# The queries of a wide cross-attention: two contexts' first, the other fourteen's inside the first chunk-maximum pass

## The chip, the cores and the metric

The kernel runs on one core of one Trainium2 chip. The metric is the device time of one execution in microseconds, the median of three runs. The engines that matter are PE (TensorE, matmuls, with PEld its weight loads), DVE (VectorE), ACT (ScalarE), POOL (GpSimd) and SP, which issues most DMAs. Each has its own instruction queue and they meet only through semaphores and at the end of a block.

## The reference, cut to what matters

Four gated layers follow each other, each a cross-attention and a feed-forward part. The change is in the cross-attention of the second layer (L1) alone. x is 32 batches of 56 queries by 128; the context of a batch is 1500 rows by 96; 16 heads of 64.

```python
q = (x @ Wq).reshape(B, Nq, h, dh)          # x: layer-normed, 32 x 56 x 128
k = (context @ Wk).reshape(B, Nk, h, dh)    # context: 32 x 1500 x 96
v = (context @ Wv).reshape(B, Nk, h, dh)
scores = einsum('bqhd,bkhd->bhqk', q, k) / sqrt(dh)
attn = softmax(scores, axis=-1)
out = einsum('bhqk,bkhd->bqhd', attn, v).reshape(B, Nq, h * dh) @ Wo + bo
```

## The kernel before, in words

`attention_wide` first folds the weights (`fold_weights`): for each head Wq and Wk become one matrix M of 128 by 97, so that a "query" of 96 numbers meets the raw context directly; N does the same for Wv and Wo. Then it runs two halves of 16 contexts each. The program text calls a context a batch.

A half has two blocks. In the first, `make_queries` makes the queries of all 16 contexts: for two stretches c of 448 columns (8 contexts) and for 16 heads, one fp32 matmul (two passes of PE each, L527) into one of eight PSUM banks; ACT copies the even heads (L544) and DVE the odd ones (L557) into `qp`, scaled and with a bias. Beside it SP issues the loads of contexts 0 and 1 (`raw`, `cn`) and POOL issues four more (`cr`, then `ch`) and fills a row of ones. A block ends when all its engines have ended.

In the second block, contexts go two at a time (`i` is the pair, `s` which of the two), in a software pipeline written out by hand:

- POOL rounds the queries to `QB` (L1255) and splits queries and keys into high and low parts (`QH` L1265, `CL` L1269, `QL` L1271). It also issues the DMA that puts a row of maxima into `QH` (`max_row`, L1276).
- First pass, `chunks` on PE (L1328): queries times rounded keys, 11 groups for a context, ten of two matmuls of 500 columns and one of one. DVE takes each group's maximum (`chunk_max`, L1509), and after 11 groups the negated maximum of the row (L1514, L1517).
- `score` (L1351 to L1353, six matmuls of 448 columns for one key tile) needs that row through `max_row`. ACT takes the exponential (L1491), `weigh` (L1365) multiplies by the context's values.
- `project` (L1336, 16 heads, two passes each) and an ACT copy (L1429) end a pair.

For the pair 0 of a half the first pass stands ahead of the loop, alone on PE, with two pairs of PSUM banks (0 and 1, 6 and 7):

```python
pe.wait_ge(S["ones_set"].sem, 2 * half + 2)
for s in range(2):
    for k in range(CG):                    # CG = 11
        chunks(0, s, k, True)
pe.wait_ge(*at("chunk_maxed", 2 * CG))
score(0, 0)
score(0, 1)
pairs(pe, body)
```

POOL, before it reaches its loop, waits for each context's 11 groups, rounds the queries of pair 1 and issues their keys' load, and only then issues the first `max_row`. From the loop's start on, the first pass of pair i + 1 lies between the scores of pair i. ACT's queue in the second block begins with two loads of a stored image and one operation on it (L1444); then it waits for the first score.

Of the kernel before, what the change touches and what calls it, by code (L numbers as in the profile page):

```python
# [19 lines left out]
ALU = mybir.AluOpType  # L20
# [3 lines left out]
B, NQ, D = 32, 56, 128  # L24
# [30 lines left out]
class Core:  # L55
# [27 lines left out]
    def new_signals(self, later=False):  # L83

        nc, old = self.nc, self.signals
        if later:
            self.done += old
        elif old:
            with nc.Block() as block:
                @block.gpsimd  # L90
                def _(pool):
                    nc.clear_and_free_semaphores([s.sem for s in old])
        self.signals = []
        self.part += 1
        self.step = {e: self.sig(f"{e}_step") for e in ("dve", "act", "pe", "pool")}
        self.queries_made, self.queries_act, self.queries_dve = (
            self.sig(f"queries_{n}") for n in ("made", "act", "dve"))
        self.gate_added = self.sig("gate_added")
        self.mean_ready = self.sig("mean_ready")
        self.centred = self.sig("centred")  # L100
        self.squared = self.sig("squared")
        self.var_ready = self.sig("var_ready")
        self.std_ready = self.sig("std_ready")
        self.inverse_ready = self.sig("inverse_ready")
        self.inverse_spread = self.sig("inverse_spread")
# [402 lines left out]
                                            ALU.mult).then_inc(m_sb.sem, 1)  # L508


def make_queries(core, qp, M, cq, src, scale, half, loads, rounded_loads):

    nc, ps = core.nc, core.ps
    qmm, qa, qd_ = core.queries_made, core.queries_act, core.queries_dve
    nch = NCH // 2
    with nc.Block() as block:
        block.sync(loads)
        block.gpsimd(rounded_loads)

        @block.tensor  # L520
        def _(pe):
            with pe.Fori(0, nch) as c:
                for h in range(H):

                    w = qa if h % 2 == 0 else qd_
                    pe.wait_ge(w.sem, w.at(8 * c + h // 2 + 1))
                    nc.tensor.matmul(ps[0:KA, h % 8, 0:CH], M[:, h, :],  # L527
                                     src[:, bass.ds(c * CH + half * nch * CH, CH)],
                                     start=True, stop=True).then_inc(qmm.sem, 1)

        def bank(h):
            return ps[0:KA, h % 8, 0:CH].rearrange("p (b q) -> p b q", q=NQ)

        def place(h, c):
            return qp[0:KA, bass.ds(c * 8, 8), h * NQ:(h + 1) * NQ]

        @block.scalar
        def _(act):
            act.sem_inc(qa.sem, 4)
            with act.Fori(0, nch) as c:  # L540
                for h in range(0, H, 2):
                    act.wait_ge(qmm.sem, qmm.at(H * c + h + 1))
                    if cq is not None:
                        ins = nc.scalar.activation(place(h, c), bank(h), ACT.Identity,  # L544
                                                   bias=cq[:, h:h + 1], scale=scale)
                    else:
                        ins = nc.scalar.activation(place(h, c), bank(h), ACT.Copy)
                    ins.then_inc(qa.sem, 1)

        @block.vector  # L550
        def _(dve):
            dve.sem_inc(qd_.sem, 4)
            with dve.Fori(0, nch) as c:
                for h in range(1, H, 2):
                    dve.wait_ge(qmm.sem, qmm.at(H * c + h + 1))
                    if cq is not None:
                        ins = nc.vector.tensor_scalar(place(h, c), bank(h), scale, cq[:, h:h + 1],  # L557
                                                      ALU.mult, ALU.add)
                    else:
                        ins = nc.vector.tensor_copy(place(h, c), bank(h))  # L560
                    ins.then_inc(qd_.sem, 1)
    qmm.base += H * nch
    qa.base += H * nch // 2 + 4
    qd_.base += H * nch // 2 + 4

PRODUCTS = [(0, 0), (0, 1), (1, 0), (1, 1), (0, 2), (2, 0)]
# [22 lines left out]
def attention_normed(core, L, qn, bo, rk, bit, image):  # L595
# [10 lines left out]
    with ExitStack() as ctx:  # L606
# [486 lines left out]
        "den_out": 32 * NP, "den_stored": 32 * NP, "den_in": 32 * NP, "den_inverted": 2 * NP,  # L1093
        "u_normed": 2 * NP + 1, "projected": NP, "out_copied": NP,
        "img_in": 96 * NP, "img_valued": 6 * NP, "img_scaled": 6 * NP, "img_rounded": 6 * NP,
        "img_made": 6 * NP, "img_kept": 6 * NP, "img_seen": 6 * NP, "img_out0": 48 * NP, "img_out1": 48 * NP}
IMAGE_AT = (1, 4, 7, 13, 16, 19)


def attention_wide(core, L, src, bo, scale, bit, image, norm):  # L1100

    outer = ExitStack()
    N = core.sb(f"{L}_N", [KA, H, D], F32, outer)
    M = core.sb(f"{L}_M", [D, H, KA], F32, outer)
    cq = core.sb(f"{L}_cq", [KA, H], F32, outer)
    S = {n: core.sig(f"{L}_{n}") for n in [*WIDE, "ones_set"]}
    with outer:
        fold_weights(core, L, M, N, cq, scale, True, 64, None, norm)
        for half in range(2):
            with ExitStack() as ctx:  # L1110
                qp = core.sb(f"{L}_qp{half}", [DC + 8, HB, HQ], F32, ctx)

                def queries(loads, rounded_loads):
                    make_queries(core, qp, M, cq, src, scale, half, loads, rounded_loads)
                attend_wide(core, f"{L}{half}", S, qp, N, bo, half, ctx, bit, image, queries)


def attend_wide(core, tag, S, qp, N, bo, half, ctx, bit, image, queries):

# [2 lines left out]

    nc, d, ps = core.nc, core.d, core.ps
    b0 = half * HB

    def at(name, n):
        return S[name].sem, S[name].at(n)

    def sb(name, shape, dt=F32):
        return core.sb(f"{tag}_{name}", shape, dt, ctx)
# [87 lines left out]
        for s in range(2):  # L1220
            nc.gpsimd.tensor_copy(CH[s][DC:KA, :], core.ones[DC:KA, 0:1].to_broadcast([1, NK])).then_inc(S["ones_set"].sem, 1)

    queries(loads, rounded_loads)
    with nc.Block() as block:
        @block.sync
        def _(sp):
            def invert(i, s):

                sp.wait_ge(*at("u_copied", 2 * i + s + 2))

                sp.dma_start(dn, UE[DC:KA, :]).then_inc(S["den_out"].sem, 16)
                sp.wait_ge(*at("den_inverted", 2 * i + s + 1))
                sp.dma_start(den.rearrange("o (t n) -> (o t) n", t=8), dr).then_inc(S["den_stored"].sem, 16)
                sp.wait_ge(*at("den_stored", 32 * i + 16 * s + 16))
                sp.dma_start(RB[:, :], den.to_broadcast([DC, HQ])).then_inc(S["den_in"].sem, 16)

            def body(i, prev, nxt, after):
                if prev:
                    invert(i - 1, 1)
                for s in range(2):  # L1240
                    if nxt:
                        sp.wait_ge(*at(f"keys_split{s}", 3 * i + 3))
                        raw_keys(sp, i + 1, s)
                        sp.wait_ge(*at("weighed", 24 * i + 12 * s + 14))
                        rows(sp, i + 1, s)
                    if s == 0:
                        invert(i, 0)

            pairs(sp, body)
            invert(NP - 1, 1)  # L1250

        @block.gpsimd
        def _(pool):
            def first_pass_inputs(i, s, keys=True):
                nc.gpsimd.tensor_copy(QB[s][:, :].rearrange("c (t p) -> c t p", p=128),  # L1255
                                      folded(i, s).rearrange("c (p t) -> c t p", p=128)
                                      ).then_inc(S[f"qb_ready{s}"].sem, 1)
                if keys:
                    first_pass_keys(pool, i, s)
# [14 lines left out]
            def max_row(i, s):  # L1274
                pool.wait_ge(*at("max_negated", 2 * i + s + 1))
                pool.dma_start(QH[s][DC:KA, :], negated(i, s)).then_inc(S[f"max_in{s}"].sem, 16)  # L1276
# [10 lines left out]
            for s in range(2):  # L1287

                pool.wait_ge(*at("chunk_scored", CG * s + CG))
                first_pass_inputs(1, s)  # L1290
            max_row(0, 0)

            def body(i, prev, nxt, after):
                max_row(i, 1)
# [18 lines left out]
        def _(pe):  # L1313
# [76 lines left out]
            def body(i, prev, nxt, after):  # L1390
                for k in range(24):
# [15 lines left out]
                    if k % KT == 0:  # L1407
                        aside(i, k, prev, nxt)
                        weigh(i, k)

            pe.wait_ge(S["ones_set"].sem, 2 * half + 2)
            for s in range(2):
                for k in range(CG):
                    chunks(0, s, k, True)
            pe.wait_ge(*at("chunk_maxed", 2 * CG))
            score(0, 0)
            score(0, 1)
            pairs(pe, body)
            pe.wait_ge(*at("u_normed", 2 * NP))
# [3 lines left out]
        def _(act):  # L1423
# [36 lines left out]
            def image_step(i, n, prev, nxt):  # L1460

                for c, k in enumerate(IMAGE_AT):
# [6 lines left out]
                    if n == k + 4 and (c < 4 or nxt):  # L1469
                        j = (i, c + 2) if c < 4 else (i + 1, c - 4)  # L1470
                        act.wait_ge(*at("img_valued", 6 * i + c + 2))
                        load_image(*j)

            load_image(0, 0)
            value(0, 0, False)
            act.wait_ge(*at("img_valued", 1))
            load_image(0, 1)

            def body(i, prev, nxt, after):
                for n in range(24):  # L1480
# [2334 lines left out]
```

## Time and profile before

| what | us |
|---|---|
| median of 3 runs (lowest, highest) | 4207.23 (4205.37, 4211.37) |
| profiled execution | 4212.35 |
| its span from first to last instruction | 4210.4 |
| PE, DVE, ACT, POOL busy in the span | 3661.9, 2545.5, 2041.4, 1477.9 |
| queries of the first half, L527, first to last matmul | 26.07 |
| queries of the second half, L527 | 26.71 |

Times within the trace count from the span's start. In a timeline row, the first two numbers are start and length; `x4` is how many instructions were merged; the bracket tells how long the engine had been idle before and what ended that. In the table of stretches, PEclk is the granted share of TensorE's full clock: 1.00 is 2.4 GHz, 0.50 is 1.2 GHz. Ends of matmuls are modelled, so the spacing of their starts is the better measure.

### The profile page before, as it was taken

Reading aid. Unit: us, or ns where it says so; the run is one execution under the profiler, and the core shown is the slowest. Engines: PE = TensorE matmul, PEld = TensorE weight load, DVE = VectorE, ACT = ScalarE, POOL = GpSimd, SP = SyncE. Lnnn points to the kernel's source line nnn. Section 1 sums busy time; section 2 is a strip of 40 time slices with the busy share of each in tenths; the row PEclk is TensorE's granted clock in tenths of the full one; section 3 lists DMA queues with packets and bytes.
Section 4 is the critical chain, followed back from the end, with each engine's and each line's share of the span. In section 5 each row is a group of like instructions: output and inputs, shape, how many; then the busy total and the mean of one; then the engine's idle time right before and its main releaser. Section 6 shows DMA issues by size and latency. Waiting matters only on the chain. (4 is left out here: it accounts for less than half of the span.)

```text
span 4210.4 us, 84369 instructions
## 1 busy us (share of the span) xinstructions
PE 3661.9 (87%) x33096; PEld 2477.5 (59%) x33096; DVE 2545.5 (60%) x3583; ACT 2041.4 (48%) x2943; POOL 1477.9 (35%) x1913
## 2 busy tenths in 40 slices
PE   8499999937489999988999997679858799999987
PEld 8267777724446666655666665357633366666664
DVE  7556666535155554525554542467644799999995
ACT  8177777701024443432443342166422477777764
POOL 5275455130423323212223220022201666666640
PEclk9599999969679999998999997889979799999998
DMA  6177777446223233221332220021000666666650
GB/s 185 48 177 178 169 176 172 120 184 231 47 70 93 82 86 85 79 66 55 85 88 85 83 76 25 9 63 48 10 19 26 138 156 154 156 155 155 155 131 25
DMA packets 201964, 436.40 MB, mean 104 GB/s; under 512 B 46666, under 2 KB 103917, under 8 KB 201517
## 3 DMA queue, kind: packets, MB, share of 16 engines
q1 hardware_dynamic: 127196, 341.47, 31.3%
q0 software_dynamic: 38944, 47.04, 5.2%
q10 hardware_dynamic: 35504, 43.39, 3.8%
q8 instruction: 230, 3.77, 0.4%
q14 instruction: 90, 0.73, 0.1%
HBM read 246.72 MB, written 32.67 MB: 66 GB/s over the span
## 5 line engine op out<-in xcount | busy, mean ns | idle before, releaser
L1509 DVE TENSOR_REDUCE L_mp<-ps 128x2 f32<-128x1000 f32 (+1 forms) x352 | 403.4, 1152 | 554.7 <-PE ps L1328 551.3
L1491 ACT ACTIVATE L_p<-ps 125x896 f32<-125x896 f32 x384 | 352.1, 917 | 606.2 <-PE ps L1353 534.5
L1365 PE MATMUL ps<-L_p,L_cn 125*97 125x448 f32 x1536 | 639.2, 538 | 0.0
L2196 ACT ACTIVATE L_p<-L_p 125x896 f32<-125x896 f32 x384 | 364.5, 950 | 226.4 <-DVE L_p L2257 222.6
L2240 DVE TENSOR_REDUCE L_mp<-ps 112x2 f32<-112x1000 f32 x384 | 455.4, 1190 | 18.2 <-PE ps L2002 18.1
L2257 DVE SCALAR_TENSOR_TENSOR L_p<-ps,xn 125x896 f32<-125x896 f32 x384 | 414.0, 1080 | 16.8 <-PE ps L2022 16.5
L1351 PE MATMUL ps<-L_qh,L_ch 97*125 97x448 f32 x768 | 385.8, 502 | 14.6 <-DMA L_qh<-L_mc 14.6
L1365 PEld LDWEIGHTS ps<-L_p,L_cn 125*97 125x97 f32 x1536 | 250.4, 163 | 199.9 <-issue 165.9
L2002 PE MATMUL ps<-L_ks,L_qs 96*128 96x500 bf16 x768 | 236.2, 392 | 78.8 <-DVE L_mp L2240 65.5
L1352 PE MATMUL ps<-L_ql,L_ch 96*125 96x448 f32 x768 | 284.0, 370 | 0.0
L1353 PE MATMUL ps<-L_qh,L_cl 96*125 96x448 f32 x768 | 282.5, 368 | 0.0
L946 ACT ACTIVATE L_p<-ps,rk 125x896 f32<-125x896 f32 x256 | 257.5, 1007 | 51.1 <-PE ps L802 46.9
L1328 PE MATMUL ps<-L_cr,L_qb 96*128 96x500 f32 x672 | 242.2, 443 | 13.3 <-DVE L_mp L1509 7.2
L1777 POOL DMA_DIRECT2D L_qs<-L_q_part x381 | 211.7, 564 | 99.4 <-PE ps L2022 93.0
L2022 PEld LDWEIGHTS ps<-L_qs,L_ks 128*128 128x128 bf16 x3072 | 188.9, 98 | 74.5 <-issue 45.2
L802 PEld LDWEIGHTS ps<-L_qs,L_ks 128*128 128x128 bf16 x3072 | 188.1, 98 | 72.9 <-issue 54.4
L2035 PE MATMUL ps<-L_p,L_vs 125*18 125x112 f32 x6144 | 223.2, 263 | 3.5 <-ACT L_p L2196 3.1
L802 PE MATMUL ps<-L_qs,L_ks 128*128 128x112 bf16 x3072 | 216.1, 213 | 3.4 <-ACT L_p L946 3.4
L728 POOL DMA_DIRECT2D L_qs<-L_q_part x384 | 214.3, 566 | 7.6 <-DVEq L1068 6.8
L2022 PE MATMUL ps<-L_qs,L_ks 128*128 128x112 bf16 x3072 | 215.1, 213 | 1.5 <-DVE L_p L2257 1.0
L1280 POOL TENSOR_TENSOR L_un<-L_ue,L_rb 96x896 f32<-96x896 f32 x32 | 67.1, 2097 | 423.6 <-DMA L_rb<-L_den 423.6
L718 POOL TENSOR_TENSOR L_k_part<-L_k_rest,L_k_part 128x500 bf16<-128x500 f32 x96 | 109.2, 1139 | 300.3 <-ACT L_k_part L911 300.2
(537 smaller groups left out, 7299.8 us busy)
## 6 DMA issues: line engine op xcount, KB each, us to landing
L_ks<-L_k_part SPq DMA_DIRECT2D x288, 375.0 KB, 6.6
L_ks<-L_k_first SPq DMA_DIRECT2D x96, 375.0 KB, 6.3
moe_w<-in_L_w SPq DMA_DIRECT2D x64, 512.0 KB, 6.6
L_cn<-in_ctxN SPq DMA_DIRECT2D x32, 568.4 KB
cs_ct<-in_ctxT SPq DMA_DIRECT2D x32, 562.5 KB, 4.2
L_raw<-in_ctxT SPq DMA_DIRECT2D x32, 562.5 KB, 4.8
L_cr<-in_ctxT POOLq DMA_DIRECT2D x32, 562.5 KB, 5.0
L_ch<-in_ctxT POOLq DMA_DIRECT2D x32, 562.5 KB, 4.5
```

Source lines behind the costliest of these rows:

```text
L802: mm = nc.tensor.matmul(SB[n % 2][:, m // 4, m % 4 * 2 * NQ:(m % 4 + 1) * 2 * NQ] .rearrange("p (j q) -> p j q", j=2), KS[b.r % 3][:, k0:k ...
L946: nc.scalar.activation(weights_at[n % 3][0:KP, :].rearrange("p (a n) -> p a n", a=2), SB[n % 2][0:KP], ACT.Exp, scale=rk[:, b.lin(KT, n):b ...
L1351: nc.tensor.matmul(SB[n % 2][:, a, :], CH[s][:, k], QH[s][:, q], start=True, stop=False)
L1352: nc.tensor.matmul(SB[n % 2][:, a, :], CH[s][0:DC, k], QL[s][:, q], start=False, stop=False)
L1353: mm = nc.tensor.matmul(SB[n % 2][:, a, :], CL[s][:, k], QH[s][0:DC, q], start=False, stop=True)
L1365: mm = nc.tensor.matmul(U[:, a, :], CN[s][:, j, :], P[:, n % 2, a * HALF:(a + 1) * HALF], start=(j == 0), stop=(j == KT - 1))
L1491: nc.scalar.activation(two(P[:, n % 2, :]), SB[n % 2], ACT.Exp).then_inc(S["exped"].sem, 1)
L1509: nc.vector.tensor_reduce(mp[:, 2 * k:2 * k + n], ps[:, bank:bank + n, 0:500], AX.X, ALU.max).then_inc(S["chunk_maxed"].sem, 1)
L2022: mm = nc.tensor.matmul(SB[n % 2][:, m // 4, m % 4 * 2 * NQ:(m % 4 + 1) * 2 * NQ] .rearrange("p (j q) -> p j q", j=2), KS[b.r % 4][:, k0:k ...
L2196: nc.scalar.activation(two(P[0:KP, n % 3, :]), two(P[0:KP, n % 3, :]), ACT.Exp).then_inc(S["exped"], 1)
L2240: nc.vector.tensor_reduce(mp[:, 2 * c:2 * c + 2], ps[0:TT, CB[pair], 0:500], AX.X, ALU.max).then_inc(S["chunk_maxed"], 1)
L2257: nc.vector.scalar_tensor_tensor(out=two(P[0:KP, n % 3, :]), in0=SB[n % 2][0:KP], scalar=0.0, in1=two(LB[0:KP, b.r % 2, :]), op0=ALU.min, ...
```

## The change

`make_queries` is replaced by `first_queries`, which in the first block makes the queries of contexts 0 and 1 only: 16 matmuls of 112 columns into banks 0 to 3, four heads to a bank, with no loop; ACT copies heads 0 to 3 and 8 to 11, DVE the others, each after its four heads. POOL's four loads and its row of ones stay in that block. SP's four loads move into the second block and wait there until `cr` of context 1 has landed.

The queries of the other 14 contexts are made in the second block by 32 matmuls of 392 columns (`late_query`, 7 contexts by 16 heads, twice). One stands behind each of the 22 chunk groups of pair 0 in PE's queue, the last ten behind those. They use banks 2 to 5; from the fifth on each waits for the copy of the one four before. ACT alone copies them, behind its image operation. The second score waits for all 32 copies; POOL waits for 16 copies before it rounds the queries of pair 1, and for all 32 before its loop. The bias row of 97 becomes 96 rows (the 97th was not used in `qp`).

```diff
-def make_queries(core, qp, M, cq, src, scale, half, loads, rounded_loads):
+def first_queries(core, S, qp, M, cq, src, scale, half, rounded_loads):
...
+            for h in range(H):
+                nc.tensor.matmul(ps[0:DC, h // 4, h % 4 * 2 * NQ:(h % 4 + 1) * 2 * NQ], M[:, h, 0:DC],
+                                 src[:, b0 * NQ:(b0 + 2) * NQ], start=True, stop=True
+                                 ).then_inc(S["early_made"].sem, 1)
...
+            for h in (h for h in range(H) if h // 4 % 2 == 0):
+                act.wait_ge(*at("early_made", h // 4 * 4 + 4))
+                nc.scalar.activation(place(h), bank(h), ACT.Identity, bias=cq[0:DC, h:h + 1], scale=scale)
...
+            for h in (h for h in range(H) if h // 4 % 2 == 1):
+                dve.wait_ge(*at("early_made", h // 4 * 4 + 4))
+                nc.vector.tensor_scalar(place(h), bank(h), scale, cq[0:DC, h:h + 1], ALU.mult, ALU.add)
...
+LATE_BATCHES = (HB - 2) // 2
...
+            sp.wait_ge(*at("ctr_in1", 16))
+            loads(sp)
...
                 pool.wait_ge(*at("chunk_scored", CG * s + CG))
+                pool.wait_ge(*at("late_copied", H))
                 first_pass_inputs(1, s)
             max_row(0, 0)
+            pool.wait_ge(*at("late_copied", 2 * H))
...
+            def late_query(e):
+                if e >= 4:
+                    pe.wait_ge(*at("late_copied", e - 3))
+                c = (b0 + late_batches(e)) * NQ
+                nc.tensor.matmul(ps[0:DC, 2 + e % 4, 0:LATE_BATCHES * NQ], M[:, e % H, 0:DC], src[:, c:c + LATE_BATCHES * NQ],
+                                 start=True, stop=True).then_inc(S["late_made"].sem, 1)
...
                     chunks(0, s, k, True)
+                    late_query(CG * s + k)
+            for e in range(2 * CG, 2 * H):
+                late_query(e)
             pe.wait_ge(*at("chunk_maxed", 2 * CG))
             score(0, 0)
+            pe.wait_ge(*at("late_copied", 2 * H))
             score(0, 1)
...
+            def copy_late_query(e):
+                act.wait_ge(*at("late_made", e + 1))
+                n, h = late_batches(e), e % H
+                nc.scalar.activation(qp[0:DC, n:n + LATE_BATCHES, h * NQ:(h + 1) * NQ],
+                                     ps[0:DC, 2 + e % 4, 0:LATE_BATCHES * NQ].rearrange("p (b q) -> p b q", q=NQ),
+                                     ACT.Identity, bias=cq[0:DC, h:h + 1], scale=scale
+                                     ).then_inc(S["late_copied"].sem, 1)
...
+            for e in range(2 * H):
+                copy_late_query(e)
```

## Rows read from the trace of the kernel before

**Rows 1.** The page, part 1: busy time and share of each engine.
```profile
PE 3661.9 (87%) x33096; PEld 2477.5 (59%) x33096; DVE 2545.5 (60%) x3583; ACT 2041.4 (48%) x2943; POOL 1477.9 (35%) x1913
```
**Rows 2.** Timeline of the first half's start: start, length, engine, line, instruction, idle before.
```profile
1163.91 26.07 PE L527 MATMUL ps<-xn,L_M 128*97 x64 [0.88 <-ACTq L539]
...
1191.11 3.57 POOL L1255 CAST L_qb<-L_qp 96x896 fp32r<-96x896 f32 x2 [22.07 <-POOLq L516]
1193.03 1.14 PE L1328 MATMUL ps<-L_cr,L_qb 96*128 96x500 f32 x4 [3.05 <-POOL L_qb L1255]
1193.75 2.31 DVE L1509 TENSOR_REDUCE L_mp<-ps 128x2 f32<-128x1000 f32 x2 [2.94 <-PE ps L1328]
...
1195.65 3.36 POOL L1269 TENSOR_TENSOR L_cl<-L_raw,L_ch 96x1500 fp32r<-96x1500 f32 x1
1196.24 2.31 DVE L1509 TENSOR_REDUCE L_mp<-ps 128x2 f32<-128x1000 f32 x2 [0.19 <-PE ps L1328]
...
1218.61 0.79 PE L1328 MATMUL ps<-L_cr,L_qb 96*128 96x500 f32 x1 [0.18 <-DVE L_mp L1509]
1219.47 1.77 POOL L1255 CAST L_qb<-L_qp 96x896 fp32r<-96x896 f32 x1 [9.83 <-PE ps L1328]
...
1226.87 0.71 PE L1351 MATMUL ps<-L_qh,L_ch 97*125 97x448 f32 x1 [7.48 <-DMA L_qh<-L_mc]
```
**Rows 3.** Timeline of the loop's first steps, PE alone.
```profile
1231.49 1.02 PE L1328 MATMUL ps<-L_cr,L_qb 96*128 96x500 f32 x2
1232.32 0.39 PE L1351 MATMUL ps<-L_qh,L_ch 97*125 97x448 f32 x1
...
1233.57 1.67 PE L1365 MATMUL ps<-L_p,L_cn 125*97 125x448 f32 x4
...
1238.51 0.61 PE L1328 MATMUL ps<-L_cr,L_qb 96*128 96x500 f32 x2
1238.96 1.67 PE L1365 MATMUL ps<-L_p,L_cn 125*97 125x448 f32 x4
```
**Rows 4.** Timeline around the start of the second half.
```profile
1867.78 7.14 PE L1336 MATMUL ps<-L_un,L_N 96*128 96x112 f32 x32 [10.15 <-POOL L_un L1280]
...
1875.99 26.71 PE L527 MATMUL ps<-xn,L_M 128*97 x64 [1.07 <-ACTq L539]
...
1903.83 3.54 POOL L1255 CAST L_qb<-L_qp 96x896 fp32r<-96x896 f32 x2 [22.90 <-POOLq L516]
```
**Rows 5.** Stretches: length, busy time of PE, PEld, DVE, ACT, POOL, PEclk, DMA share, GB/s.
```profile
1163.50:1167.50 4.00, 3.59 (x5) 1.55 (x6) 0.11 (x1) 0.63 (x1) 3.42 (x5) 0.50 0.74 187
1167.50:1190.00 22.50, 22.48 (x60) 9.51 (x58) 10.16 (x15) 9.50 (x15) 1.53 (x2) 1.00 0.72 173
1195.00:1219.00 24.00, 21.64 (x38) 9.74 (x38) 22.44 (x22) 0.96 (x1) 14.47 (x8) 0.50 0.19 54
1227.00:1232.00 5.00, 5.00 (x14) 4.38 (x15) 0.00 (x0) 1.19 (x2) 0.00 (x0) 0.50 0.00 0
1867.00:1875.00 8.00, 7.14 (x32) 6.90 (x32) 0.00 (x0) 0.04 (x1) 0.64 (x1) 0.50 0.00 0
3600.00:3700.00 100.00, 92.25 (x1345) 61.56 (x1336) 98.46 (x102) 70.45 (x112) 59.89 (x106) 1.00 0.71 161
1232.00:1840.00 608.00, 608.00 (x2413) 408.93 (x2412) 296.11 (x381) 248.91 (x346) 161.74 (x109) 1.00 0.28 79
```
**Rows 6.** Groups by line: busy, mean ns of one, idle before.
```profile
L544 ACT ACTIVATE L_qp<-ps,L_cq 97x448 f32 x32 | 20.3, 633 | 59.5 <-PE ps L527 59.5
L1429 ACT ACTIVATE OT<-ps,vec 128x112 f32 (+1 forms) x16 | 5.7, 353 | 94.3 <-PE ps L1336 94.3
L1018 DVE SCALAR_TENSOR_TENSOR OT<-ps,vec,OT 128x112 f32<-128x112 f32 x16 | 5.2, 323 | 3.5 <-PE ps L843 3.5
```
**Rows 7.** DMA issues at 1163.9, and at 1209: count, KB, us to landing.
```profile
L_cr<-in_ctxT POOLq DMA_DIRECT2D x1, 562.5 KB, 11.1
...
L_cr<-in_ctxT POOLq DMA_DIRECT2D x1, 562.5 KB, 4.5
```

More of the change, by code:

```diff
@@ L95, in new_signals @@
         self.step = {e: self.sig(f"{e}_step") for e in ("dve", "act", "pe", "pool")}
-        self.queries_made, self.queries_act, self.queries_dve = (
-            self.sig(f"queries_{n}") for n in ("made", "act", "dve"))
         self.gate_added = self.sig("gate_added")
@@ L508, in _, with at, bank, place @@
                                             ALU.mult).then_inc(m_sb.sem, 1)
-def make_queries(core, qp, M, cq, src, scale, half, loads, rounded_loads):
+def first_queries(core, S, qp, M, cq, src, scale, half, rounded_loads):
     nc, ps = core.nc, core.ps
-    qmm, qa, qd_ = core.queries_made, core.queries_act, core.queries_dve
-    nch = NCH // 2
+    b0 = half * HB
+    def at(name, n):
+        return S[name].sem, S[name].at(n)
+    def bank(h):
+        return ps[0:DC, h // 4, h % 4 * 2 * NQ:(h % 4 + 1) * 2 * NQ].rearrange("p (b q) -> p b q", q=NQ)
+    def place(h):
+        return qp[0:DC, 0:2, h * NQ:(h + 1) * NQ]
     with nc.Block() as block:
-        block.sync(loads)
         block.gpsimd(rounded_loads)
@@ L521, in _ @@
         def _(pe):
[L522 to L532, printed above, removed]
@@ L534, in place @@
-        def place(h, c):
-            return qp[0:KA, bass.ds(c * 8, 8), h * NQ:(h + 1) * NQ]
+            for h in range(H):
+                nc.tensor.matmul(ps[0:DC, h // 4, h % 4 * 2 * NQ:(h % 4 + 1) * 2 * NQ], M[:, h, 0:DC],
+                                 src[:, b0 * NQ:(b0 + 2) * NQ], start=True, stop=True
+                                 ).then_inc(S["early_made"].sem, 1)
         @block.scalar
         def _(act):
[L539 to L548, printed above, removed]
+            for h in (h for h in range(H) if h // 4 % 2 == 0):
+                act.wait_ge(*at("early_made", h // 4 * 4 + 4))
+                nc.scalar.activation(place(h), bank(h), ACT.Identity, bias=cq[0:DC, h:h + 1], scale=scale)
@@ L550, in _ @@
         @block.vector
         def _(dve):
[L552 to L561, printed above, removed]
@@ L562, in make_queries @@
-    qmm.base += H * nch
-    qa.base += H * nch // 2 + 4
-    qd_.base += H * nch // 2 + 4
+            for h in (h for h in range(H) if h // 4 % 2 == 1):
+                dve.wait_ge(*at("early_made", h // 4 * 4 + 4))
+                nc.vector.tensor_scalar(place(h), bank(h), scale, cq[0:DC, h:h + 1], ALU.mult, ALU.add)
 PRODUCTS = [(0, 0), (0, 1), (1, 0), (1, 1), (0, 2), (2, 0)]
@@ L1095 @@
         "img_in": 96 * NP, "img_valued": 6 * NP, "img_scaled": 6 * NP, "img_rounded": 6 * NP,
+        "early_made": H, "late_made": 2 * H, "late_copied": 2 * H,
         "img_made": 6 * NP, "img_kept": 6 * NP, "img_seen": 6 * NP, "img_out0": 48 * NP, "img_out1": 48 * NP}
 IMAGE_AT = (1, 4, 7, 13, 16, 19)
+LATE_BATCHES = (HB - 2) // 2
 def attention_wide(core, L, src, bo, scale, bit, image, norm):
@@ L1111, in attention_wide, with attend_wide, late_batches @@
                 qp = core.sb(f"{L}_qp{half}", [DC + 8, HB, HQ], F32, ctx)
[L1113 to L1118, printed above, removed]
+                attend_wide(core, f"{L}{half}", S, qp, (M, cq, src, scale), N, bo, half, ctx, bit, image)
+def attend_wide(core, tag, S, qp, query, N, bo, half, ctx, bit, image):
     nc, d, ps = core.nc, core.d, core.ps
     b0 = half * HB
+    M, cq, src, scale = query
     def at(name, n):
         return S[name].sem, S[name].at(n)
+    def late_batches(e):
+        return 2 + LATE_BATCHES * (e // H)
     def sb(name, shape, dt=F32):
@@ L1221, in rounded_loads @@
             nc.gpsimd.tensor_copy(CH[s][DC:KA, :], core.ones[DC:KA, 0:1].to_broadcast([1, NK])).then_inc(S["ones_set"].sem, 1)
-    queries(loads, rounded_loads)
+    first_queries(core, S, qp, M, cq, src, scale, half, rounded_loads)
     with nc.Block() as block:
```

## The prediction

> **What bounds the kernel now.** I read the shares of the engines first. PE is busy for 87% of the span [rows 1], so the question for any stretch is whether PE is the bound there, and at which clock. The table of stretches answers it [rows 5]: from 1232 to 1840, the loop of the first half, PE is busy 608.00 of 608.00 us at PEclk 1.00. In the loop only less PE work saves time, and the change takes none out of it. The rest I read from the timeline ahead of the loop, because that is where the edit lies.
>
> There the kernel is serial. In the first half PE makes queries from 1163.91 on, and POOL, which needs only the first two contexts' queries, begins to round them at 1191.11, when the whole block has ended [rows 2]: 27.20 us. In the second half it is 1875.99 to 1903.83 [rows 4]: 27.84 us. PE sets this stretch: 60 passes fill 22.48 of 22.50 us, 0.375 us each, at clock 1.00 [rows 5].
>
> Behind it comes the first pass of pair 0, 1193.03 (first chunk matmul) to 1226.87 (first score), 33.84 us. Here the end is set by DVE and by PE's latency in turn: two maxima take 2.31 us, then DVE idles 0.19 us for PE, and the next two start 2.49 us after the first (1193.75, 1196.24) [rows 2]. The clock is 0.50 from 1195 to 1219 [rows 5]. A pair of chunk matmuls takes 0.83 us there (that of 1231.49 to 1232.32, still at the low level) and 0.45 us at the high one (1238.51 to 1238.96) [rows 3]. So at 1.2 GHz PE has work for 0.83 of each 1.25 us, and ACT and SP have next to none: ACT is busy 0.96 us of 24 [rows 5]. The last chunk starts at 1218.61; then POOL rounds once more (1219.47, 1.77 us), issues `max_row`, and PE idles 7.48 us before the score [rows 2].
>
> **The change, part by part.**
>
> *First block.* Removed per half: 27.20 and 27.84 us. In its place 16 matmuls of 112 columns, 32 passes. `project` has just these, 32 passes of 112 columns in 7.14 us [rows 4], at clock 0.50 [rows 5]. I take 7.14, since the block starts at 0.50 [rows 5] and `project` did not raise the clock in as much time. Copies of three groups of heads lie beside PE; the last group's four by DVE come after it, at 0.323 us each, the nearest row with 112 columns read from PSUM [rows 6]: 1.29. ACT's last four end earlier: 0.353 each [rows 6], begun a quarter of 7.14 us before. Hand-over costs about 0.3 us on both sides of them (an estimate: 0.72 us from chunk to maximum [rows 2] less 0.45 for the pair [rows 3]). Sum 7.14 + 1.29 + 0.6 = 9.0. Gain 18.2 and 18.8 us. Bounds: passes at half that price (3.6), or at the 0.407 us of a full pass (26.07/64 [rows 2], 13.0 in all): 5.9 us less to 3.5 us more gain in a half.
>
> *Loads.* `cr` of context 0 landed 11.1 us after its issue when it shared the DMA engines with SP's four loads; alone it takes 4.5 [rows 7]. Now SP's stand behind it, so it lands near 1169, before the rounded queries (9.0 + 1.8 us after 1163.91, about 1174.7). If it still took 11.1 it would land at 1175.2 and cost 0.5. `raw` starts some 10 us later; POOL wants it for `CL` 4.5 us after its first rounding [rows 2]. Even a late `raw` delays only POOL's splitting: 14.47 us of POOL work between 1195 and 1219 [rows 5], the later rounding included, wanted by a score 33 us after the first chunk. Cost 0.
>
> *Chunks with 22 late queries among them.* A late query is two passes of 392 columns: 2 x 0.375 x 392/448 = 0.66 us at clock 1.00, 1.31 at 0.50. With its chunk pair PE needs 1.11 us a group at 2.4 GHz, 2.14 at 1.2. So the clock decides. What raises it in this trace: full-width passes back to back, after 4 us in the query block (0.50 to 1167.5, then 1.00) and after 5 us of scores (0.50 to 1232, then 1.00); what keeps it: 92.25% busy from 3600 to 3700 at 1.00 [rows 5]. With a query behind each group PE has no pause at 1.2 GHz, so I expect the rise after 4 to 5 us and then 1.00. In those, PE does two groups, where DVE did 3.5; I put the loss at 2.4 us. Then PE (1.11) and DVE (1.11 when maxima run back to back: 2.31 for two with 1.20 for the last) go level, against 1.25 before: 18 full groups by 0.14 win 2.5 back. Net next to nothing; I book a loss of 0.3 us. Bounds: a gain of 2, and the first rival.
>
> *Tail.* The query behind the last group and the ten after it are 11 x 0.66 = 7.2 us. POOL's round and `max_row` hide it: the score came 7.48 us after PE's last chunk [rows 2]. Nothing moves, with some 0.5 us to spare. ACT's copies lie between 0.353 (112 columns) and 0.633 us (448) [rows 6], by the line through both 0.59 for 392, below PE's 0.66, four banks deep. Were the tail at 1.2 GHz it would take 14.4 and cost 7 a half. POOL's added wait for 16 copies ends with group 16, before its wait for 22; its wait for 32 holds back only the `max_row` of the second context, needed twelve key tiles later.
>
> *Scores that start at full clock.* PE no longer idles for 7 us before the first score. The twelve matmuls of the first two scores and the chunk pair behind them took 1226.87 to 1232.32, 5.45 us, at clock 0.50 [rows 2, 3, 5]. In the loop six scores take 1.25 us (1232.32 to 1233.57) and the pair 0.45 [rows 3]: 2.95 us. Gain at most 2.5, I take 2.3; zero if the clock falls.
>
> *Sum.* First half 18.2 - 0.3 + 2.3 = 20.2, second 20.8: 41.0 us. The profiled execution took 4212.35 us, so 4171.3 for it; it lay 5.1 over the median of the runs, and against the median the same step gives 4207.23 - 41.0 = 4166.2.
>
> **The rivals.**
>
> *The clock stays low (slower).* Between 1195 and 1219 PE counts as 21.64 us busy of 24 and had 0.50 all the while [rows 5], so a nearly busy PE is not proof of a high clock. If it stays at 1.2 GHz until the first score, PE is the bound: 20 groups of 2.14, two short ones of 1.73, ten queries of 1.31, 59.4 us where 33.84 were: +25.5 a half. Against 18.2 and 18.8 that is 14 us slower, 4221. It decides from about seven tenths of the phase at 1.2 GHz on. Against it: the same trace rises in every stretch where full-width matmuls stand without pauses. The Trainium skill ("TensorE: Matmul & The Clock Gate", "A second HAM failure mode: psum-queue depth-cycling") reports a kernel that, going round PSUM banks, paused so often that its clock fell and rose again and again; by that rule this is the case. The 92% of 3600 to 3700 speak against it here.
>
> *The clock is high only in part.* It rises late or falls once, for instance when PE meets DVE's pause at the change of context, and the tail or a third of the phase runs at 1.2 GHz: 7 to 9 us a half. Gain 23 to 27, about 4182. For it: level PE and DVE leave no reserve.
>
> *The gain is given back.* Something that the long query block covers becomes the wait, such as the contexts that SP reads later, or the image load ahead of ACT's copies in the same DMA traffic, and all of it is lost: 4207. Priced by the 11.1 us of a load in traffic [rows 7], ACT begins to copy some 3 us after PE wants its first bank back, 3 us a half, far from all; and the loop behind, PE from end to end, gives back nothing.
>
> **How the numbers follow.** Forecast 4166, chance 0.70, its own range 4156 to 4176 (bounds of the first block and no gain in the scores). Clock in part 0.14; slower by the clock 0.06; given back or not done 0.05; a larger gain, by a faster first block, 0.05. Differences under 0.2% (8.4 us) can't be told from none. Faster 0.89, the same 0.05, slower 0.06. The range of 8 in 10 reaches into the partial clock: 4156 to 4187.
>
> **What would show it.** Right: POOL's first rounding about 9 us after the first query matmul; PEclk 1.00 from some 5 us after the first chunk; maxima 1.1 to 1.2 us apart; first score 33 to 35 us after the first chunk, its matmuls 0.2 us apart; the loop as long as before. Wrong: 0.50 in the chunk stretch, chunk groups 2 us apart, a score that waits for copies rather than for `max_row`, or a first block of over 13 us.

## The result, and the profile after

The changed kernel takes 4169.23 us (4166.84 to 4173.88) against 4208.06 (4205.37 to 4211.37) for the one before on the same chip: ratio 0.9905, interval [0.9894, 0.9917]. The forecast was 4166, faster. The sum is near, but its largest term was not: errors of both signs partly cancel.

The timeline of the changed kernel at the first half's start, engine by engine, in the columns of [rows 2]:

```profile
1159.77 5.17 PE L529 MATMUL ps<-xn,L_M 128*96 128x112 f32 x32 [0.53 <-PEq L468]
...
1164.99 1.06 DVE L543 TENSOR_SCALAR L_qp<-ps,L_cq 96x112 f32<-96x112 f32 x4 [0.84 <-PE ps L529]
1171.95 0.34 SPq L1172 DMA_DIRECT2D L_raw<-in_ctxT  x1
1171.96 3.52 POOL L1235 CAST L_qb<-L_qp 96x896 fp32r<-96x896 f32 x2 [6.71 <-POOLq L523]
...
1173.88 1.17 PE L1310 MATMUL ps<-L_cr,L_qb 96*128 96x500 f32 x2 [8.93 <-POOL L_qb L1235]
...
1177.23 10.84 DVE L1512 TENSOR_REDUCE L_mp<-ps 128x2 f32<-128x1000 f32 x10 [0.94 <-PE ps L1310]
...
1199.11 0.55 PE L1310 MATMUL ps<-L_cr,L_qb 96*128 96x500 f32 x1
1199.50 7.41 PE L1397 MATMUL ps<-xn,L_M 128*96 128x392 f32 x22
1202.06 0.58 POOL L1256 DMA_DIRECT2D L_qh<-L_mc  x1
1206.80 0.44 PE L1333 MATMUL ps<-L_qh,L_ch 97*125 97x448 f32 x1
...
1211.13 1.67 PE L1347 MATMUL ps<-L_p,L_cn 125*97 125x448 f32 x4
```

Three things are to be seen. The queries and their copies are done at 1166.05, and no engine computes until 1171.95, when SP, ACT and POOL all start: the block's end is late. From 1177.23 ten maxima, the last of half width, run in one row of 10.84 us, almost without a wait for PE; full ones start 1.11 to 1.12 us apart. And PE goes from its last late query into the first score with no idle time shown ahead of it, where it had 7.48 us before [rows 2].

What held the block's end is in the view of one line, the one that opens the block: its queue instructions, with shortest, median and longest length in ns, first and last start. First the changed kernel, then the one before:

```profile
L523 POOLq DRAIN  x2: 10087/10136/10185, 1161.6 to 1854.8; - x2
L523 DVEq DRAIN  x2: 1067/1068/1069, 1165.0 to 1858.1; - x2
```
```profile
L516 POOLq DRAIN  x2: 19431/19522/19614, 1165.4 to 1877.3; - x2
```

At a block's end every engine has a DRAIN. POOL's lasts 10.1 us in the changed kernel and ends at 1171.7, 5.7 us after the last copy and 0.2 us after POOL's last load landed (1171.50). In the kernel before it was longer, 19.6 us in this half, to 1185.0, again 0.2 us after POOL's last load landed (1184.81), but it ended 6 us ahead of the query copies, and nothing showed. There SP's loads were still moving until 1188.2, so it was POOL's own loads that the drain waited for.

The stretches of the changed kernel, in the columns of [rows 5]:

```profile
1163.70:1167.10 3.40, 1.25 (x13) 1.06 (x11) 1.50 (x6) 1.07 (x4) 1.55 (x2) 1.00 1.19 268
1165.00:1173.80 8.80, 0.00 (x0) 0.00 (x0) 1.04 (x4) 0.29 (x2) 2.08 (x3) 0.62 0.78 178
1167.10:1177.30 10.20, 3.42 (x7) 2.29 (x8) 1.27 (x2) 0.05 (x1) 4.75 (x4) 0.50 0.78 193
1173.80:1176.00 2.20, 2.12 (x5) 1.40 (x5) 0.91 (x1) 0.00 (x0) 2.20 (x2) 0.50 1.06 287
1178.00:1199.00 21.00, 20.83 (x75) 12.25 (x74) 20.89 (x22) 11.50 (x21) 13.00 (x7) 1.00 0.34 106
1199.00:1206.80 7.80, 7.80 (x26) 3.79 (x24) 3.31 (x7) 6.34 (x11) 2.90 (x3) 1.00 0.42 100
1211.00:1820.00 609.00, 609.00 (x2415) 409.17 (x2414) 296.33 (x383) 250.13 (x348) 163.71 (x109) 1.00 0.28 79
```

PEclk is 0.50 in the first 3.4 us of chunks, to 1177.3, and 1.00 from there through tail and scores; PE and DVE are both busy for 99% of 1178 to 1199. The clock had been at 1.00 once already, from 1163.7 in the first queries, and fell at 1167.1, while PE stood idle behind the late block end. The loop is what it was [rows 5].

Four marks on the timelines, the first query matmul, the first rounding, the first chunk, the first score, and the first `weigh` as the end, give this account, both halves added (us):

| stretch | before | after | difference | forecast |
|---|---|---|---|---|
| first query to first rounding | 27.20 + 27.84 | 12.19 + 12.17 | -30.7 | -37.0 |
| first rounding to first chunk | 1.92 + 1.92 | 1.92 + 1.91 | 0.0 | 0 |
| first chunk to first score | 33.84 + 35.18 | 32.92 + 33.85 | -2.3 | +0.6 |
| first score to first `weigh` | 6.70 + 6.40 | 4.33 + 4.22 | -4.6 | -4.6 |
| all | 141.0 | 103.5 | -37.5 | -41.0 |

The two profiled spans differ by 45.2 us (4210.4 and 4165.2); 4.1 of that lies ahead of the first query (1163.91 and 1159.77), where the program is the same, and 3.6 in the loops and behind them. Both are within what executions of one kernel differ by here (4205.37 to 4211.37).

### The profile page after: what moved, and what is told of

Read it like the earlier page. It is cut to its first block and busy times, and to the rows that moved or that the text cites. A ratio compares the mean times of both kernels' runs of the same rounds, so it can differ in the third digit from the quotient of the medians.

```text
span 4165.2 us, 84341 instructions
## 1 busy us (share of the span) xinstructions
PE 3629.1 (87%) x33160; PEld 2475.5 (59%) x33160; DVE 2526.5 (61%) x3567; ACT 2062.2 (50%) x2991; POOL 1478.7 (36%) x1913
```

## The experiments

Each kernel ran beside the kernel before on the same chip. That one's median was 4208.06 us beside the changed kernel, 4205.96 beside the first four experiments and 4209.73 beside the last three, so medians taken beside different ones of these compare to within 2 to 4 us only. Where it matters, the four marks of the profiled executions stand beside them; numbers for a half are from these marks.

**SP's loads early.** Is the drain a fixed cost, and does "contexts read later" matter?

```diff
     with nc.Block() as block:
+        block.sync(loads)
         block.gpsimd(rounded_loads)
...
-            sp.wait_ge(*at("ctr_in1", 16))
-            loads(sp)
```

> The changed kernel, but SP issues its four loads in the first block, beside POOL's, as the kernel before did. Theory: the four loads of POOL then land 19 to 21 us after their issue, as before the change; the drain waits for that, and the second block starts near 1181 in place of 1172: 18 us slower in all, 4187. Rival: the drain has its own length of 10 us, only `cr` is late (11.1 us, within it): 4169, the later reading of contexts is worth nothing.

Measured 4186.45 us, ratio 0.9954 [0.9941, 0.9968]. The drain and the first chunk (two views):

```profile
L523 POOLq DRAIN  x2: 19892/19924/19955, 1163.8 to 1866.3; - x2
```
```profile
1185.96 1.17 PE L1308 MATMUL ps<-L_cr,L_qb 96*128 96x500 f32 x2 [19.07 <-POOL L_qb L1233]
```

The same four loads of POOL, and the drain is twice as long, because SP's traffic slows them. The rounding begins 22.1 and 21.9 us after the first query in place of 12.2, 19.6 us in all. By the marks up to the first `weigh` 17.8 of it remain, because the chunks take 2.1 us less; by the medians it is 17, and against the kernel before this one gains 19.5 us where the changed kernel gains 38.8. So the drain follows the loads, and the edit that looked like a detail, SP's loads behind `cr`, is worth 17 to 19 of the 39 us.

**`ch` later.** Then fewer loads should shorten the drain.

```diff
         for s in range(2):
             first_pass_keys(pool, 0, s)
-        for s in range(2):
-            high_keys(pool, 0, s)
...
-                split_keys(0, s, False)
+                split_keys(0, s)
```

> The changed kernel, but POOL issues the two `ch` loads in the second block, each ahead of its key split, and only the two `cr` loads in the first. Theory: the end of the first block waits for POOL's DRAIN, and that lasts until every load POOL has issued has landed (in the changed kernel 10.1 us, to 1171.8, 5.7 us after the last copy of queries at 1166.05). With two loads in place of four the drain ends 4 to 5 us sooner, and so does POOL's first rounding after the first query matmul (7.5 to 8.5 us in place of 12.2); 8 us less in all, 4161. Rival: a drain after POOL's DMAs has a length of its own, some 10 us; then the rounding still begins 12 us after the first query matmul and the time stays at 4169.

Measured 4173.43 us, ratio 0.9925 [0.9912, 0.9939]: not faster than the changed kernel (0.9905). The step held, the time did not follow. The drain, and then POOL and PE behind it:

```profile
L523 POOLq DRAIN  x2: 6358/6402/6447, 1160.3 to 1855.0; - x2
```
```profile
1166.87 3.53 POOL L1233 CAST L_qb<-L_qp 96x896 fp32r<-96x896 f32 x2 [3.14 <-POOLq L523]
...
1179.56 3.38 POOL L1247 TENSOR_TENSOR L_cl<-L_raw,L_ch 96x1500 fp32r<-96x1500 f32 x1 [7.73 <-DMA L_ch<-in_ctxT]
...
1191.24 3.38 POOL L1247 TENSOR_TENSOR L_cl<-L_raw,L_ch 96x1500 fp32r<-96x1500 f32 x1 [4.83 <-DMA L_ch<-in_ctxT]
...
1201.19 0.57 POOL L1254 DMA_DIRECT2D L_qh<-L_mc  x1
1206.42 0.44 PE L1331 MATMUL ps<-L_qh,L_ch 97*125 97x448 f32 x1 [3.59 <-DMA L_qh<-L_mc]
...
1902.95 0.71 PE L1331 MATMUL ps<-L_qh,L_ch 97*125 97x448 f32 x1 [6.83 <-DMA L_qh<-L_mc]
```
```profile
1208.14:1211.55 3.41, 3.41 (x11) 2.92 (x10) 0.90 (x1) 1.61 (x2) 0.00 (x0) 0.50 0.00 0
1901.05:1907.80 6.75, 4.85 (x13) 4.33 (x14) 0.00 (x0) 0.92 (x1) 0.00 (x0) 0.50 0.03 1
```

The rounding begins 7.6 us after the first query, 4.6 sooner. But POOL now waits 7.73 and 4.83 us for `ch`, comes late to its rounding for pair 1 and to `max_row`, and PE idles 3.59 and 6.83 us for that row. From first chunk to first score it takes 37.6 and 39.4 us in place of 32.9 and 33.9. Behind these idle stretches the clock is at 0.50, and the scores up to the first `weigh` take 5.7 and 6.4 us in place of 4.3 and 4.2. So 9.2 us won ahead of the rounding stand against 10.2 and 3.6 lost behind it: 4.7 us slower by the marks, 4.2 by the medians. The wait was moved, not removed: both `ch` loads stand in POOL's own queue, the second behind the first context's whole split.

**One block.** The drain taken away altogether; the copies are awaited by semaphores.

```diff
-    first_queries(core, S, qp, M, cq, src, scale, half, rounded_loads)
+    make_early, copy_early_act, copy_early_dve, early_copied = first_queries(core, S, qp, M, cq, src, scale, half)
...
+            rounded_loads(pool)
+            early_copied(pool)          # 8 copies of ACT, 8 of DVE
             for s in range(2):
                 first_pass_inputs(0, s, False)
...
+            make_early(pe)
             pe.wait_ge(S["ones_set"].sem, 2 * half + 2)
+            early_copied(pe)
...
+            copy_early_act(act)
             load_image(0, 0)
...
+            copy_early_dve(dve)
```

> The changed kernel with the first queries moved into the second block: no block end between them and the first rounding, POOL and PE wait for the sixteen copies by semaphores instead. Theory: the 5.7 us between the last copy and the first rounding go, in each half: rounding 6.5 us after the first query matmul, 11 us less in all, 4158. Rival: the wait comes back as a wait for `cr` or `raw`, which now share the DMA engines sooner; then first chunk or first score stand where they did and the gain is under 4 us.

Measured 4160.11 us, ratio 0.9891 [0.9876, 0.9906]. The rounding begins 6.3 and 6.4 us after the first query, so the 5.8 us a half are gone, 11.6 in all. By the medians 9 of the expected 11 us arrive, by the marks 6.5: from first chunk to first score it takes 34.5 and 37.0 us in place of 32.9 and 33.9. In the second half of this kernel:

```profile
1872.00 3.38 POOL L1251 TENSOR_TENSOR L_cl<-L_raw,L_ch 96x1500 fp32r<-96x1500 f32 x1 [0.28 <-POOL L_qh L1247]
...
1873.05 2.35 DVE L1527 TENSOR_SCALAR L_mc<-L_mu 128x7 f32<-128x7 f32 x1
...
1876.56 0.88 PE L1314 MATMUL ps<-L_cr,L_qb 96*128 96x500 f32 x2 [1.73 <-DVE L_mp L1519]
```
```profile
1876.96:1880.38 3.42, 3.42 (x9) 1.97 (x7) 2.52 (x3) 0.58 (x1) 0.45 (x1) 0.50 0.09 35
```

That operation on 7 elements a partition, in the turn from the first context's maxima to the second's, took 0.79 and 0.17 us in the changed kernel. It ends at 1875.40, together with the POOL operation that runs beside it (1875.37); the last section comes back to this. PE then waits 1.73 us for DVE, and the clock falls to 0.50 for 3.4 us.

**The kernel before with the late matmuls added.** Is the clock the cause of what was won behind the first block?

```diff
                 for k in range(CG):
                     chunks(0, s, k, True)
+                    filler(CG * s + k)       # late_query's matmul, not read, no wait
+            for e in range(2 * CG, 2 * H):
+                filler(e)
             pe.wait_ge(*at("chunk_maxed", 2 * CG))
```

> The kernel before, with all queries in the first block, and the changed kernel's 32 late matmuls added at the same places of PE's queue, into banks 2 to 5; their results are not read. It is PE work added and nothing taken out. Theory: they raise the clock, and so the stretch from first chunk to first score stays at 33 to 34 us and the scores behind it take 3.0 us in place of 5.45: 4 to 7 us faster than before, 4202, although PE has 26 us more to do. Rival: what the changed kernel won behind its first block is not due to the clock; then the filler is neutral or adds its time, 4208 or more.

Measured 4201.27 us, ratio 0.9988 [0.9978, 0.9997]. Stretches, then the first score and the first `weigh`:

```profile
1198.00:1220.00 22.00, 20.83 (x74) 12.02 (x73) 21.83 (x24) 0.00 (x0) 11.74 (x9) 1.00 0.19 52
1220.00:1227.00 7.00, 6.68 (x25) 3.92 (x24) 0.12 (x1) 0.57 (x1) 0.88 (x2) 1.00 0.39 83
```
```profile
1224.94 0.43 PE L1351 MATMUL ps<-L_qh,L_ch 97*125 97x448 f32 x1 [0.32 <-DMA L_qh<-L_mc]
...
1229.12 1.29 PE L1365 MATMUL ps<-L_p,L_cn 125*97 125x448 f32 x3
```

PEclk is 1.00 where it was 0.50 [rows 5]. First chunk to first score takes 34.3 us in each half (33.8 and 35.2 before), and the scores to `weigh` 4.2 us in place of 6.70 and 6.40: 64 passes of PE, about 21 us of work at the high clock, were added in each half (42 in both, where the expectation says 26) and the kernel became 5 us faster; the interval allows 1 to 9. By the marks 4.7 us of it lie behind the first score.

**`max_row` first.** What sets the first score, PE's tail or the row?

```diff
                 pool.wait_ge(*at("chunk_scored", CG * s + CG))
+                if s == 0:
+                    max_row(0, 0)
                 pool.wait_ge(*at("late_copied", H))
                 first_pass_inputs(1, s)
-            max_row(0, 0)
```

> The changed kernel, but POOL issues `max_row` of the first context as soon as its maxima are there, between the two roundings for pair 1, and no longer behind the second of them and its key load. Theory: what sets the first score is PE's own tail of eleven late queries (1199.50 to 1206.80, then the score with no idle time), so an earlier row changes nothing: first score 33 us after the first chunk, 4169. Rival: the row's DMA (issued at 1202.06, landed 4.5 us later) sets it; then the score comes sooner and 2 to 4 us go.

Measured 4167.13 us, ratio 0.9901 [0.9887, 0.9915], the same as the changed kernel. The row goes out 16.0 us after the first chunk in place of 28.2, and the score, as before, follows the tail without idle time:

```profile
1191.54 0.59 POOL L1256 DMA_DIRECT2D L_qh<-L_mc  x1 [0.63 <-PE ps L1311]
...
1201.35 7.41 PE L1398 MATMUL ps<-xn,L_M 128*96 128x392 f32 x22
1208.29 0.67 PE L1334 MATMUL ps<-L_qh,L_ch 97*125 97x448 f32 x1
```

From the last chunk to the first score it takes 7.35 and 7.47 us, in the changed kernel 7.69 and 7.71. So the row held the score back by some 0.3 us there, and with the row out of the way PE's tail is the bound. The prediction gave the tail 0.5 us to spare inside the row's way; the two are all but even.

**DVE copies every second late query.**

```diff
                 for k in range(CG):
                     chunk_max(0, s, k, True)
+                    if (CG * s + k) % 2:
+                        copy_late_query(CG * s + k)
```

> The changed kernel, but DVE copies every second late query, behind the maximum of its group (two counters in place of one). Theory: DVE is level with PE in the chunk stretch (maxima back to back, 1.11 us), so its 11 copies there, 0.6 us each by the 0.684 us of 448 columns, lengthen it by 6.5 us a half, 13 in all, 4182; ACT alone costs nothing there. Rival: PE is the bound and DVE has time between its maxima, then under 3 us.

Measured 4178.51 us, ratio 0.9927 [0.9915, 0.9939]: 9 us slower than the changed kernel. DVE, and PE waiting for it:

```profile
1184.80 0.61 DVE L1529 TENSOR_SCALAR L_qp<-ps,L_cq 96x392 f32<-96x392 f32 x1
1185.34 2.29 DVE L1515 TENSOR_REDUCE L_mp<-ps 128x2 f32<-128x1000 f32 x2
...
1186.58 0.72 PE L1312 MATMUL ps<-L_cr,L_qb 96*128 96x500 f32 x2 [0.27 <-DVE L_mp L1515]
```

Two groups take 2.75 us (copies at 1184.80 and 1187.55) in place of 2.2, 0.5 us for each copy of 0.61. The last chunk comes 4.6 and 4.1 us later than in the changed kernel, not 6.5: the mechanism holds, the measured size is a third smaller.

**The better version.** One block, two late queries in the time in which PE waits for the rounding, `max_row` first, the first image load ahead of ACT's copies.

```diff
             make_early(pe)
+            for e in range(AHEAD):             # AHEAD = 2
+                late_query(e)
...
-                    late_query(CG * s + k)
+                    late_query(AHEAD + CG * s + k)
...
+            load_image(0, 0)
             copy_early_act(act)
-            load_image(0, 0)
```

> The one-block kernel with three more changes: PE makes two late queries while it waits for POOL's first rounding (3.15 us idle in the one-block kernel), so that nine in place of eleven stand in the tail; `max_row` of the first context goes out as soon as it can; ACT issues the first image load ahead of its copies. Theory: PE is the bound from the first chunk to the first score; two queries of 0.66 us leave that stretch, and the clock rises some 2.6 us of work sooner (about 2 us less at 1.2 GHz): 3 to 4 us a half, 4153. Rival: the two queries run at 1.2 GHz, 1.31 us each, delay the first chunk, and the clock rises no sooner: 4160 as without them.

Measured 4147.75 us (4141.75 to 4156.14), ratio 0.9864 [0.9849, 0.9879], faster than both kernels. Its timeline and one stretch:

```profile
1154.32 5.12 PE L525 MATMUL ps<-xn,L_M 128*96 128x112 f32 x32 [0.53 <-PEq L468]
1159.28 1.48 PE L1403 MATMUL ps<-xn,L_M 128*96 128x392 f32 x4
1160.67 3.55 POOL L1238 CAST L_qb<-L_qp 96x896 fp32r<-96x896 f32 x2 [0.88 <-DVE L_qp L538]
1162.61 0.69 PE L1316 MATMUL ps<-L_cr,L_qb 96*128 96x500 f32 x2 [1.85 <-POOL L_qb L1238]
...
1192.29 0.67 PE L1339 MATMUL ps<-L_qh,L_ch 97*125 97x448 f32 x1
```
```profile
1158.00:1165.00 7.00, 5.15 (x27) 3.37 (x27) 3.41 (x9) 3.40 (x8) 6.12 (x5) 0.99 1.16 253
```

The two queries take 1.48 us, at the high clock, and the clock no longer falls before the chunks (0.99 from 1158 to 1165). First chunk to first score is 29.7 and 29.6 us in place of 32.9 and 33.9, first query to first `weigh` 42.7 and 43.1 in place of 51.4 and 52.2: 17.8 us less by the marks, 21 by the medians. Against the one-block kernel it is 12 us by the medians and 11 by the marks, where 7 were expected; that kernel's long DVE operations (1.56 and 2.35 us, here 0.86 and 0.82) and the fall of its clock are in the difference. What each of the three additions brings was not measured apart.

## Why the prediction was right, and which step of it was not

*First block: the direction right, the size wrong.* The step that failed is "hand-over costs about 0.3 us on both sides". It was taken from a hand-over inside a block, but this is the end of one. POOL's drain waited for the four loads, and the hand-over took 5.9 us (1166.05 to 1171.95), 6.1 in the second half. In the kernel before the same wait stood in the trace as a drain of 19.5 us in POOL's queue, hidden by 27 us of queries: the cover was removed, and I had not asked what else it covered. The loads early, `ch` later and the single block show it from three sides (drains of 19.9, 6.4 us and none). The prediction's sentence that `cr` lands early enough was true; it is `ch`, which nobody needed yet, that counted. A smaller error lay the other way: the 32 passes took 5.17 us, not 7.14, and a group's four DVE copies 1.06, not 1.29. Both things in which the passes differ from `project` count. The stationary matrix is 128 rows by 96 columns here and 96 by 128 there: at PEclk 0.50 the passes start 0.187 us apart here and 0.213 there. And the clock rose at 1163.7, which the prediction had ruled out by `project`: from there on they start 0.096 us apart. Over 32 passes the first makes some 0.8 us (32 x 0.026, an estimate), the clock the remaining 1.1. Net 12.2 us against 9.0.

*Chunks with late queries: right, with a small gain missed.* The clock was at 1.00 after 3.4 us, two groups, in the first half and after 6.5 us, four groups, in the second; 4 to 5 us were expected. Then DVE's maxima are back to back, 1.11 us apart. From first chunk to first score both halves together won 2.3 us where 0.6 was booked as a loss. The second half before had a long DVE operation of the kind named above, 1.83 us; that is about 1.2 of it, an estimate against the 0.59 us of the first half.

*Scores at full clock: right.* -4.6 us as booked, and the filler shows by itself that the clock is the cause: with it alone, the scores fall by 2.2 to 2.5 us a half.

*Tail: right that it costs nothing, but closer than said.* By the prediction's own rows the spare was 0.3 us (7.48 less 7.2), not 0.5, and in the second half before PE idled only 7.11 us, so there was none. The first score comes 7.7 us after the last chunk in each half, 8.3 and 7.9 before; tail and row end within 0.3 us of each other, as `max_row` first shows.

*ACT's copies and POOL's waits: right.* ACT needs 0.58 us a copy (0.59 in the prediction), less than the 0.66 us in which PE makes a query in the tail, and no wait of PE for a copy shows. POOL did idle 5.5 and 5.9 us for the sixteenth copy, ahead of its first rounding for pair 1; no wait of PE behind it comes from that. The copies on DVE show what the choice of ACT is worth: 9 us.

*The rivals.* For the changed kernel the clock that stays low and the clock that is high in part are both out: 1.00 from 1177.3 in the first half and from 1873.6 in the second, up to the end of the loop. The second of them was no idle thought: in the one-block kernel the clock did fall once, where PE met DVE's pause at the change of context, as that rival says. "TensorE: Matmul & The Clock Gate" of the Trainium skill, "A second HAM failure mode: psum-queue depth-cycling", reports a clock that falls and rises again where PE, going round banks, pauses often. Here PE goes round eight banks but is 99% busy from 1178 to 1199, and the trace shows one rise and no fall. "The gain is given back" named the right kind of thing, a wait that the long query block had covered, and the wrong place: not a late context, but the block's end waiting for contexts that came early. It took 11.4 us of the gain (5.9 and 6.1 less the 0.3 booked in each half), not all.

*Luck.* That the total came within 3 us is partly luck. By the marks the block's end cost 11.4 us more than booked; cheaper query passes and copies gave back 5.1 of it, and the chunk stretch 2.9, where a small loss had been booked. The forecast of the first block alone was 6.3 us off.

## What to carry to other kernels

When a stage that hides things is shortened, list everything that ends inside its time, queue instructions and block ends too: the POOL drain was in the old trace, 6 us short of mattering. A load issued early by POOL isn't free if its block ends early. Of the two remedies tried here, merging the blocks won 6.5 to 9 us, and issuing loads in the block that uses them won nothing, because they then stood in the way of POOL's later work. Where PE pauses in a stretch at the low clock, work of full width put into the gaps can cost less than nothing: 21 us of PE work in each half brought 5 us in all.

## What the hardware showed that I had not expected

With loads of its own in flight, POOL's DRAIN at a block's end lasts until they have landed: 19.5, 10.1, 19.9 and 6.4 us with four loads in traffic, four alone, four in traffic again, two alone. In the first three the trace has the landings, and the drain ends 0.2 us after the last of them. With two loads it has not, but their last packet ends 0.6 us ahead of the drain, as in the changed kernel. Without such loads it isn't free either. At the end of the loop's block before, with none in flight, it took 5.8 us and ended 3.7 us after POOL's last operation:

```profile
L1224 POOLq DRAIN  x2: 5773/5775/5777, 1865.5 to 2579.5; - x2
```

A DVE operation on 7 elements a partition took from 0.17 to 2.35 us, at the same place in the program, in different halves and kernels. The traces show what it waits for. In the second half of the kernel before:

```profile
1920.06 1.80 POOL L1255 CAST L_qb<-L_qp 96x896 fp32r<-96x896 f32 x1
1920.07 1.83 DVE L1517 TENSOR_SCALAR L_mc<-L_mu 128x7 f32<-128x7 f32 x1
```

It ends 0.03 us after the POOL operation beside it, at 1921.90. The nine traces hold 576 of these operations. In 279 it took over 0.2 us, and each of those ends 0.03 to 0.04 us after a POOL operation that ran beside it; the 293 with no POOL operation beside them took 0.17 us, as did four that met only the end of one. So POOL's work can hold DVE with no semaphore between them, and the statement at the start, that the engines meet only through semaphores and at the end of a block, is too strong. No experiment moved POOL's operation alone to test this.
